# Chunked causal linear attention with a routed expert layer: a reordered start, the state's part of y as two products with q stationary behind y's transposes, and the state by column tiles

## The chip, the core and the metric

The kernel runs on one core of one Trainium2 chip, as one launch. The metric is the device time of that launch in microseconds (us), the median over runs. The core has a matrix engine (PE, with its weight loads listed apart as PEld), a vector engine (DVE), a scalar engine (ACT), a general engine (POOL) and SyncE (SP), which here only issues DMAs. The engines run their own instruction streams in order and meet at semaphores. Each stream of this kernel is written by hand, so what stands behind a waiting instruction on its engine waits too.

## The reference

`x` is 4 sequences of 1024 tokens of width 256. After a layer norm, three things are added: `x` itself, a causal linear attention with 16 heads of width 16, and a top-1 routed expert layer (8 experts, 256 to 1024 to 256).

```python
xn = _layernorm(x, axis=-1)
x = x + _L0_attn_ref(xn, w_attn, w_proj) + _L0_ffn_ref(xn, gate_w, gate_b, expert_bias, w1, b1, w2, b2)
...
q, k, v = jnp.split(qkv, 3, axis=2)                  # phi(a) = elu(a) + 1 is applied to q and k
def step(carry, blk):                                # over chunks of 128 tokens
    S, z = carry
    q_c, k_c, v_c = blk
    scores = jnp.einsum('bhcd,bhkd->bhck', q_c, k_c)
    scores = jnp.where(mask, scores, 0.0)
    num = jnp.einsum('bhck,bhke->bhce', scores, v_c) + jnp.einsum('bhcd,bhde->bhce', q_c, S)
    den = scores.sum(-1) + jnp.einsum('bhcd,bhd->bhc', q_c, z)
    S = S + jnp.einsum('bhkd,bhke->bhde', k_c, v_c)
    z = z + k_c.sum(axis=2)
    return ((S, z), (num, den))
y = num / (den[..., None] + 1e-06)
```

The expert layer picks one expert per token and adds `relu(xn @ w1[e] + b1[e]) @ w2[e] + b2[e]`.

## The kernel before

**Stages.** The kernel has three stages. In the first, from 0 to 20.6 us, the attention weights `wall` (WF in the code) are squared, summed over all rows on PE, and an exponent for their scale (SV) is derived; WF is then written as a high and a low float16 part (WA). The second stage is a software pipeline over 32 chunks of 128 tokens (4 sequences of 8 chunks, `CPB` = 8), whose step p works on chunks p to p-5; it also converts the expert weights to float16 pairs (two quarters a step: `w_max` on DVE, `w_scale` and `w_hi` on ACT, `w_lo` on POOL) and finds the routing. The third, from about 298 us to the end, is the expert layer: 39 slots, gathered, multiplied and scattered. The change leaves the third stage as it is.

**A chunk c in the second stage.** POOL and DVE normalise it (`sums`, `na`, `nn_begin`, `nn_end`, `nb`), ACT and POOL split it into float16 parts (`xh` L1051, `xl` L1204), PE transposes them (`xt` L359), ACT copies (`xTc` L1057), and PE multiplies to q and k with features on the partitions (`qk` L376) and to v and the gate (`vg` L392). ACT and DVE apply phi (`relu` L1065, `exp` L1069, `phi` L707, into QK), PE transposes k (`ktr` L399), POOL masks q to even and odd heads (`km` L1211). PE forms the scores (`scores` L416, 8 products in float32 on strips of 32 rows, four banks), DVE masks them (`s_mask` L713, four times), and PE multiplies with v into bank 5 with the head's 16 outputs and its denominator on the partitions (`pv` L445, 16 products on strips of 32 columns). ACT copies that to YT1 (`y1` L1094), PE transposes it to tokens on the partitions (`yt1` L472, bank 2), DVE divides (`y` L729, L731, L735), PE transposes back (`yt2` L478), ACT copies (`y2` L1100), PE projects (`pr` L486), DVE adds the residual (`res` L741).

**The state.** The running state of a sequence is kept in bank 6. `st` (L459) adds k transposed times v: two products of the full 128 by 128 array with 136 columns, so that blocks of different heads are computed too. DVE copies it times a head mask to T32 (`t32` L722). `inter` (L429) adds the state's part to y in bank 5: four products, T32 stationary and q streaming (128 columns each). It stands in front of `pv` of the same chunk, which adds to the same bank. The first chunk of a sequence has no `inter`, the last no `st`: 28 of each.

**Order.** One step p of PE runs: `scores(p-3)`, `st(p-3)`, `ktr(p-2)`, `xt(p-1)`, `yt1(p-4)`, `inter(p-3)`, `qk(p-1)`, `yt2(p-4)`, `vg(p-1)`, `pr(p-4)`, `pv(p-3)`. In every fourth step two small products for an expert's scale are added: `mx` (L511) before `yt1` and `mxa` (L521) before `qk`. One step of DVE runs: `phi(p-2)`, two `s_mask(p-3)`, `largest` in every fourth step, `y(p-4)`, `scale` in every fourth step, two `s_mask(p-3)`, `t32(p-3)`, `nb(p)`, `w_max`, a routing piece, `res(p-4)`, `sums` and `na` for chunk p+2, `w_max`. A step of ACT ends with `y2(p-4)`, `xh(p)`, `relu(p-1)`, `exp(p-1)`. POOL runs `km(p-2)`, then in even steps `nn_end` (eight instructions on 128 by 2 elements), `w_lo`, `xl(p)`, `w_lo`, and in odd steps `nn_begin`.

## Time and profile before

| what | value |
|---|---|
| median of 3 runs | 521.93 us (519.39 to 522.41) |
| the profiled execution's own time | 522.73 us, span 520.9 us |
| PE busy | 484.3 us, 93% of the span |
| DVE busy | 405.9 us, 78% |
| ACT busy | 279.2 us, 54% |
| POOL busy | 271.6 us, 52% |
| first stage, until `qk(0)` starts | 20.58 us |
| 27 steps, `qk` start 42.74 to 255.84 | 213.10 us, 7.89 us a step |
| mean granted TensorE clock | 0.971 |

An instruction's row gives its start, its duration, the engine, the line of the code, and in brackets how long the engine had been idle before it and who ended that. Durations on PE overlap, because the matmuls are pipelined: what one of a row of products costs is the distance from its start to the next one's. The chain of waits, listed in order of time, has this distance as its second column. A float32 product appears as two records, so that x8 are four products; a transpose of float32 appears as one, and float16 as one.

### The profile page before, as it was taken

Reading aid. Unit: us, or ns where it says so; the run is one execution under the profiler, and the core shown is the slowest. Engines: PE = TensorE matmul, PEld = TensorE weight load, DVE = VectorE, ACT = ScalarE, POOL = GpSimd, SP = SyncE. Lnnn points to the kernel's source line nnn. Section 1 sums busy time; section 2 is a strip of 40 time slices with the busy share of each in tenths; the row PEclk is TensorE's granted clock in tenths of the full one; section 3 lists DMA queues with packets and bytes.
Section 4 is the critical chain, followed back from the end, with each engine's and each line's share of the span. In section 5 each row is a group of like instructions: output and inputs, shape, how many; then the busy total and the mean of one; then the engine's idle time right before and its main releaser. Section 6 shows DMA issues by size and latency. Waiting matters only on the chain.

```text
span 520.9 us, 17449 instructions
## 1 busy us (share of the span) xinstructions
PE 484.3 (93%) x6071; PEld 395.8 (76%) x6071; DVE 405.9 (78%) x885; ACT 279.2 (54%) x535; POOL 271.6 (52%) x469
## 2 busy tenths in 40 slices
PE   4489999999999999999997499999999999999996
PEld 1378888788887888778875388888888888888884
DVE  2778889999899998999878547767768676677775
ACT  0346888788778787878885033333333333333331
POOL 3444766667766677766754533443534534433322
PEclk9679999999999999999998789999999999999999
DMA  8413556566466565573452431222122212220000
GB/s 272 156 57 99 164 172 211 162 190 202 154 205 179 175 205 179 159 223 129 161 166 102 142 93 62 69 66 79 59 63 72 66 57 82 63 69 23 28 15 1
DMA packets 34160, 62.88 MB, mean 121 GB/s; under 512 B 5661, under 2 KB 10014, under 8 KB 33952
## 3 DMA queue, kind: packets, MB, share of 16 engines
q1 hardware_dynamic: 29088, 49.17, 29.7%
q0 software_dynamic: 4992, 12.60, 8.0%
q8 instruction: 55, 0.90, 0.7%
q14 instruction: 25, 0.20, 0.1%
HBM read 51.00 MB, written 13.50 MB: 124 GB/s over the span
## 4 chain that ended last, share of the span: by engine, by line
PE 82%; DVE 5%; POOL 4%; issue 4%; ACT 3%; DMA 2%; DVEq 0%; POOLq 0%; ACTq 0%
PE ps L601 20%; PE ps L614 20%; PE ps L376 7%; PE ps L416 6%; PE ps L445 5%; PE ps L486 5%; PE ps L459 4%; PE ps L429 3%; PE ps L392 3%; PE ps L472 2%; PE ps L570 2%; PE ps L399 1%; PE ps L359 1%; PE ps L349 1%; PE ps L478 1%
## 5 line engine op out<-in xcount | busy, mean ns | idle before, releaser
L601 PEld LDWEIGHTS ps<-AR,W 128*128 x1872 | 131.6, 99 | 40.0 <-issue 1.1
L601 PE MATMUL ps<-AR,W 128*128 128x128 f16 x1872 | 155.9, 221 | 0.9 <-ACT AR L1148 0.9
L614 PE MATMUL ps<-W,ST 128*128 x624 | 150.4, 326 | 0.3 <-DVE ST L1008 0.3
L1157 ACT ACTIVATE ST<-ST 128x512 f16<-128x512 f32 x78 | 49.2, 630 | 112.0 <-DVE ST L996 107.3
L996 DVE SCALAR_TENSOR_TENSOR ST<-ps,TAs,B1S 128x512 f32<-128x512 f32 x78 | 58.4, 748 | 51.5 <-PE ps L601 48.3
L1305 POOL DMA_INDIRECT out<-AR x39 | 39.8, 1021 | 103.9 <-DVE AR L1028 99.6
L1245 POOL TENSOR_TENSOR W<-ST,W 128x512 f16<-128x512 f32 x64 | 74.3, 1161 | 28.8 <-ACT W L1107 28.1
L713 DVE TENSOR_TENSOR AR<-ps,CT 128x512 f32<-128x512 f32 x128 | 82.0, 683 | 4.4 <-PE ps L416 4.2
L1300 POOL DMA_INDIRECT AR<-scr,AR x39 | 49.9, 1279 | 34.6 <-issue 14.3
L1008 DVE SCALAR_TENSOR_TENSOR ST<-ST 128x512 f16<-128x512 f32 x78 | 53.6, 687 | 15.7 <-ACT ST L1157 15.3
L376 PE MATMUL ps<-xT,WA 128*128 128x128 f16 x768 | 50.7, 225 | 3.1 <-ACT xT L1057 3.1
L376 PEld LDWEIGHTS ps<-xT,WA 128*128 128x128 f16 x768 | 46.7, 101 | 4.7 <-ACT xT L1057 4.4
L614 PEld LDWEIGHTS ps<-W,ST 128*128 128x128 f16 x624 | 48.3, 98 | 2.0 <-issue 0.4
L1115 ACT ACTIVATE ST<-ST,SC 128x512 f32<-128x512 f32 x64 | 46.4, 725 | 0.0
L1148 ACT ACTIVATE AR<-ps 128x512 f16<-128x512 f16 x39 | 23.2, 595 | 41.5 <-PE ps L570 39.3
L1204 POOL TENSOR_TENSOR XR<-AR,XR 128x256 f16<-128x256 f32 x32 | 23.4, 732 | 38.8 <-ACT XR L1051 38.8
L748 DVE TENSOR_REDUCE MX<-ST 128x1 f32<-128x512 f32 x64 | 42.6, 665 | 0.0
L1211 POOL TENSOR_TENSOR AR<-AR,CT 128x512 f32<-128x512 f32 x32 | 33.3, 1042 | 16.0 <-DVE AR L707 15.8
L1107 ACT ACTIVATE W<-ST 128x512 f16<-128x512 f32 x64 | 40.4, 631 | 1.1
L416 PE MATMUL ps<-AR 32*128 32x256 f32 x512 | 38.1, 412 | 1.0 <-DVE XR L741 1.0
L486 PE MATMUL ps<-AR 128*128 128x256 f32 x128 | 35.1, 397 | 3.0 <-ACT AR L1100 3.0
L445 PE MATMUL ps<-AR 128*32 128x128 f32 x1024 | 35.4, 280 | 0.0
(149 smaller groups left out, 765.9 us busy)
## 6 DMA issues: line engine op xcount, KB each, us to landing
ST<-in_w SPq DMA_DIRECT2D x128, 256.0 KB, 4.2
scr<-XR SPq DMA_DIRECT2D x32, 256.0 KB, 2.2
XR<-in_x SPq DMA_DIRECT2D x32, 128.0 KB, 4.6
AR<-in_b SPq DMA_DIRECT2D x1, 1024.0 KB, 5.0
AR<-in_wall SPq DMA_DIRECT2D x1, 776.0 KB, 4.5
AR<-scr,AR POOLq DMA_INDIRECT x39, 3.6
out<-AR POOLq DMA_INDIRECT x39
ST<-in_cst SPq DMA_DIRECT2D x1, 576.0 KB, 4.9
```

Source lines behind the costliest of these rows:

```text
L376: a = e.matmul(PS[0][:, j * 128:(j + 1) * 128], WA[:, wl, k, j * 128:(j + 1) * 128], x_part(c, xl_, k), start=(n == 1), stop=(n == 6))
L416: a = e.matmul(PSC[r][:, g * 256:(g + 1) * 256], QK[c % 2][rows, 256 + g * 128:384 + g * 128], QM[c % 2][rows, g], start=True, stop=True)
L445: a = e.matmul(PS[5][32 * b:32 * b + 32, j * 128:(j + 1) * 128], V32[c % 2][:, 8 * g + 4 * i + b, :], S32[2 * i + t][:, (2 * g + o) * 128: ...
L486: a = e.matmul(PS[2][:, 256:512], YT2[:, k * 128:(k + 1) * 128], WPF[:, k, :], start=(k == 0), stop=(k == 1))
L601: a = e.matmul(dst, W[:, off:off + 57472][:, bass.ds(place_of(s), 128)], XT16[s % 2][:, xl * 256 + k * 128:xl * 256 + (k + 1) * 128], star ...
L614: a = e.matmul(PS[4 + s % 2][:, 0:w], src[h % 4][:, fs], W[:, off:off + 57344 + w][:, bass.ds(place_of(s), w)], start=(f == 0 and w == 512 ...
L713: e.tensor_tensor(S32[r].rearrange("p (b n) -> p b n", b=4), PSC[r][:, :].rearrange("p (b n) -> p b n", b=4), msk, ALU.mult).then_inc(s_[r ...
L996: e.scalar_tensor_tensor(H32[h % 2].rearrange("p (f n) -> p f n", f=4), PS[h % 4][:, :].rearrange("p (f n) -> p f n", f=4), TAs[:, :, 0][: ...
L1008: e.scalar_tensor_tensor(HL2[h % 4], H32[h % 2], 0.0, HH[h % 4], ALU.max, ALU.subtract).then_inc(v_hl, 1)
L1157: e.activation(HH[h % 4], H32[h % 2], ACT.Relu).then_inc(a_hh, 1)
L1245: e.tensor_tensor(lo_, src, hi, ALU.subtract).then_inc(p_wlo, 1)
L1300: e.indirect_dma_start(XG[s % NG], None, scr, bass.IndirectOffsetOnAxis(ids[:, s:s + 1], 0), bounds_check=NT - 1, oob_is_err=False).then_i ...
```

## The change

**The start.** The first two chunks of `x` are loaded before the weights, and the weights in two halves with a semaphore each. DVE squares one half and ACT the other, to bfloat16, and PE sums them in bfloat16 with a stationary of ones in that type. The maximum is one reduction over two neighbouring banks, and the exponent is found in three more instructions instead of eight. WA is written in two pieces (columns 0 to 511 for `qk`, 512 to 775 for `vg`). `nb(0)` stands ahead of the reduction.

**The state.** `st` is now eight products of 34 columns on strips of 32 array columns, which leave out the blocks between different pairs of heads, and it stands behind `pv` at the end of the step. `t32` spreads the 34 columns over four blocks times a mask that has a DMA of its own (MH), and runs one step later.

**The state's part of y.** `inter` is now two products with q stationary and T32 streaming (136 columns each), which add to bank 2 behind `yt1` of the same chunk, one step later than before. `y` waits for it. Since q lives longer, it has three buffers (QT) beside two for k (KK). `pv` no longer adds to `inter`'s result.

```diff
-            e.dma_start(WF, wall).then_inc(d_wall, 16)
             load_x(0)
+            load_x(1)
+            for k in range(2):
+                e.dma_start(WF[:, k, :], wall[:, k, :]).then_inc(d_wall[k], 16)
             e.dma_start(CT[:, :], cst).then_inc(d_cst, 16)
-            load_x(1)
             e.dma_start(TRI, tri).then_inc(d_tri, 16)
+            e.dma_start(MH, cmh).then_inc(d_mh, 16)
...
-            e.wait_ge(p_ones, 1)
-            e.wait_ge(v_sq, 1)
-            for n0, n1, bank in ((0, 512, 3), (512, 776, 4)):
-                for k in range(2):
-                    a = e.matmul(PS[bank][:, 0:n1 - n0], ONF, SQ[:, k, n0:n1], start=(k == 0), stop=(k == 1))
+            e.wait_ge(p_one16, 1)
+            for k in range(2):
+                if k == 0:
+                    e.wait_ge(v_sq, 1)
+                else:
+                    e.wait_ge(a_sq, 1)
+                for i in range(2):
+                    a = e.matmul(PS[3 + i][:, 0:388], one16[:, :], SQ[:, k, i * 388:(i + 1) * 388],
+                                 start=(k == 0), stop=(k == 1))
             a.then_inc(t_sq, 1)
...
                 e.wait_ge(S["t32"], n_state(c - 1))
-                e.wait_ge(S["y1"], c)
                 for g in range(2):
-                    for i in range(2):
-                        j = 2 * g + i
-                        a = e.matmul(PS[5][:, j * 128:(j + 1) * 128], T32[:, g, 4 * i:4 * i + 4, :],
-                                     QK[c % 2][:, g * 128:(g + 1) * 128], start=(j == 0), stop=True,
-                                     skip_group_check=True)
+                    a = e.matmul(PS[2][:, g * 256:(g + 1) * 256].rearrange("p (h e) -> p h e", h=8)[:, :, 0:17],
+                                 QT[c % 3][:, g * 128:(g + 1) * 128], T32[:, g], start=False, stop=True,
+                                 skip_group_check=True)
                 a.then_inc(S["in"], 1)
...
                 for g in range(2):
-                    a = e.matmul(PS[6][:, g * 136:(g + 1) * 136], KT32[c % 2][:, g * 128:(g + 1) * 128],
-                                 V32[c % 2][:, 8 * g:8 * g + 8, 0:17], start=(c % CPB == 0 and g == 0),
-                                 stop=True, skip_group_check=True)
+                    for b in range(4):
+                        h = 8 * g + 2 * b
+                        a = e.matmul(PS[6][32 * b:32 * b + 32, g * 34:(g + 1) * 34],
+                                     KT32[c % 2][:, g * 128 + 32 * b:g * 128 + 32 * b + 32],
+                                     V32[c % 2][:, h:h + 2, 0:17], start=(c % CPB == 0 and g == 0),
+                                     stop=True, skip_group_check=True)
                 a.then_inc(S["st"], 1)
...
                 if on(p - 3):
                     scores(p - 3)
-                    st(p - 3)
...
                 if on(p - 4):
                     yt1(p - 4)
-                if on(p - 3):
-                    inter(p - 3)
+                    inter(p - 4)
...
                 if on(p - 3):
                     pv(p - 3)
+                    st(p - 3)
...
-                e.tensor_tensor(T32[:, :, :, 0:17], PS[6][:, 0:272].rearrange("p (g h e) -> p g h e", g=2, h=8),
+                if c == 0:
+                    e.wait_ge(d_mh, 16)
+                e.tensor_tensor(T32.rearrange("p g (b h) e -> p g b (h e)", b=4),
+                                PS[6][:, 0:68].rearrange("p (g o n) -> p g o n", g=2, o=1).broadcast_to((128, 2, 4, 34)),
                                 mh, ALU.mult).then_inc(S["t32"], 1)
...
                 e.wait_ge(S["yt1"], c + 1)
+                if n_inter(c) > 0:
+                    e.wait_ge(S["in"], n_inter(c))
...
                     s_mask(p - 3, 3)
-                    t32(p - 3)
+                if on(p - 4):
+                    t32(p - 4)
...
+                if p == 0:
+                    e.wait_ge(v_sv, 1)
+                    wa_hi(slice(0, 512))
                 if on(p - 1):
+                    if p == 1:
+                        e.wait_ge(v_sv, 2)
                     relu(p - 1)
                     exp(p - 1)
```

On PE, one step of the pipeline, from `pv` to the next `qk`, read before as follows (ps5 and ps2 are the banks of y, ps6 that of the state; L445 is `pv`, L416 `scores`, L459 `st`, L399 `ktr`, L472 `yt1`, L429 `inter`, L376 `qk`):

```order
L445 MATMUL ps<-AR 32x128 [waits s_s0,s_s1,s_y1,s_vh]
...
L416 MATMUL ps<-AR 128x256 [waits s_s2,s_s3,s_s1,s_res,s_s0,s_km]
L416 MATMUL ps<-AR 128x256 x7
L459 MATMUL ps<-AR 128x136 [waits s_t32,s_vh,s_kt]
L459 MATMUL ps<-AR 128x136
L399 MATMUL ps<-CT,AR 128x128 [waits s_phi]
...
L472 MATMUL ps<-CT,AR 128x128 [waits s_res,s_s0,s_y1]
L472 MATMUL ps<-CT,AR 128x128 x3
L429 MATMUL ps<-AR 128x128 [waits s_y1,s_t32]
L429 MATMUL ps<-AR 128x128 x3
L376 MATMUL ps<-xT,WA 128x128 [waits s_kt,s_xTc]
```

The same stretch of PE after the change (L461 is `pv`, L478 `st`, L435 `scores`, L418 `ktr`, L492 `yt1`, L445 `inter`, L393 `qk`):

```order
L461 MATMUL ps<-AR 32x128 x7
L478 MATMUL ps<-AR 32x34 [waits s_t32,s_vh,s_kt]
L478 MATMUL ps<-AR 32x34 x7
L435 MATMUL ps<-AR 128x256 [waits s_s2,s_s3,s_s1,s_res,s_s0,s_km]
L435 MATMUL ps<-AR 128x256 x7
L418 MATMUL ps<-CT,AR 128x128 [waits s_phi]
...
L492 MATMUL ps<-CT,AR 128x128 [waits s_res,s_s0,s_y1]
L492 MATMUL ps<-CT,AR 128x128 x3
L445 MATMUL ps<-AR 128x8x17 [waits s_t32]
L445 MATMUL ps<-AR 128x8x17
L393 MATMUL ps<-xT,WA 128x128 [waits s_kt,s_xTc]
```

`st` has moved from between `scores` and `ktr` to between `pv` and `scores`; `inter` has two rows' worth of products fewer and no wait for `y1`.

On DVE, the middle of a step after the change (L729 is `s_mask`, L750 to L756 are `y`, L740 is `t32`, L673 `nb`):

```order
L729 TENSOR_TENSOR AR<-ps,CT 128x512 [waits s_pv,s_sc] x2
L750 TENSOR_SCALAR DN<-ps 128x16 [waits s_in,s_yt1]
L752 RECIPROCAL DN<-DN 128x16 [waits dv]
L756 TENSOR_TENSOR AR<-ps,DN 128x256 [waits s_yt2,dv]
L729 TENSOR_TENSOR AR<-ps,CT 128x512 [waits s_pv,s_sc] x2
L740 TENSOR_TENSOR AR<-ps,AR 128x272 [waits s_in,s_st]
L673 TENSOR_SCALAR AR<-XR,mv,rsn 128x256 [waits s_xl,s_nn]
```

The order of kinds is that of before; new is that the first instruction of `y` waits for `inter` (s_in) as well as for `yt1`.

On DVE at the program's start, after the change (L660 and L667 are `sums` and `na` of chunks 0 and 1, L673 is `nb(0)`, L686 the reduction of the sums of squares, L699 the low part of WA):

```order
L660 BN_STATS st<-XR 128x6 [waits s_na,d_x1]
L667 BN_AGGR mv<-st 128x2 [waits s_sums]
L682 TENSOR_TENSOR AR<-AR 128x776 [waits d_wall0]
L673 TENSOR_SCALAR AR<-XR,mv,rsn 128x256 [waits s_nn]
L686 TENSOR_REDUCE nv<-ps 128x1 [waits t_sq]
L689 TENSOR_SCALAR nv<-nv 128x1 [waits dv]
L691 TENSOR_SCALAR ni<-nv 128x1 [waits dv]
L694 TENSOR_SCALAR SV<-ni 128x1 [waits dv]
L696 TENSOR_SCALAR SV<-SV 128x1 [waits v_sv]
L699 SCALAR_TENSOR_TENSOR WA<-AR,SV,WA 128x2x512 [waits a_wa]
L699 SCALAR_TENSOR_TENSOR WA<-AR,SV,WA 128x2x264 [waits a_wa]
```

Before, the squares of the whole WF stood first, then `sums` and `na`, the two reductions, eight small instructions, `nb(0)`, and one low part of all 1552 columns.

## Rows read from the trace of the kernel before

**Rows 1.** The page, part 1: busy us (share of the span) xinstructions
```profile
PE 484.3 (93%) x6071; PEld 395.8 (76%) x6071; DVE 405.9 (78%) x885; ACT 279.2 (54%) x535; POOL 271.6 (52%) x469
```

**Rows 2.** Chain of waits, one step of PE: start us, us to the next
```profile
121.71 1.34 PE ps L376 x24
...
124.88 1.01 PE ps L445 x32
...
126.96 0.66 PE ps L459 x4
...
128.07 0.45 PE ps L472 x4
128.51 0.89 PE ps L429 x8
```

**Rows 3.** Windows between starts of qk: length, busy us (count) by engine, clock, DMA
```profile
74.06:97.39 23.33, 22.35 (x307) 18.38 (x307) 21.70 (x50) 18.34 (x39) 15.29 (x30) 1.00 0.60 184
97.39:137.51 40.12, 40.09 (x539) 33.95 (x540) 37.16 (x91) 32.57 (x67) 28.59 (x66) 1.00 0.62 192
```

**Rows 4.** Timeline of DVE, one step: start us, us, line, operands, idle before
```profile
118.68 0.68 DVE L707 SCALAR_TENSOR_TENSOR AR<-ps,AR 128x512 f32<-128x512 f32 x1
...
120.85 0.17 DVE L729 TENSOR_SCALAR DN<-ps 128x16 f32<-128x16 f32 x1 [0.23 <-PE ps L472]
...
123.23 1.21 DVE L656 TENSOR_SCALAR AR<-XR,mv,rsn 128x256 f32<-128x256 f32 x1
...
126.41 0.68 DVE L707 SCALAR_TENSOR_TENSOR AR<-ps,AR 128x512 f32<-128x512 f32 x1
```

**Rows 5.** Line L656 (nb): ns min/median/max; and its last long one, timeline
```profile
L656 DVE TENSOR_SCALAR AR<-XR,mv,rsn x32: 400/403/1230, 15.1 to 257.4; 128x256 f32<-128x256 f32 x32
...
249.66 1.21 DVE L656 TENSOR_SCALAR AR<-XR,mv,rsn 128x256 f32<-128x256 f32 x1
```

**Rows 6.** Chain of waits, mxa (L521) ahead of a qk
```profile
137.21 0.31 PE ps L521 x2
```

**Rows 7.** Chain of waits in the first stage
```profile
0.74 4.53 DMA AR<-in_wall
...
7.22 5.53 PE ps L349 x8
12.77 0.69 DVE nv L665
...
15.24 1.59 ACT WA L1047
...
20.58 2.76 PE ps L376 x24
23.36 0.70 ACT AR L1065
```

**Rows 8.** Timeline of the first stage: na(1), end of nn_end, WA's low part, nb(1)
```profile
8.20 0.18 DVE L650 BATCH_NORM_AGGREGATE mv<-st 128x2 f32<-128x6 f32 x1
...
12.12 0.20 POOL L1182 TENSOR_TENSOR rsn<-rsn,nr 128x2 f32<-128x2 f32 x1
...
16.86 1.83 DVE L684 SCALAR_TENSOR_TENSOR WA<-AR,SV,WA 128x1552 f16<-128x1552 f32 x1 [1.34 <-ACT WA L1047]
...
20.45 0.49 DVE L656 TENSOR_SCALAR AR<-XR,mv,rsn 128x256 f32<-128x256 f32 x1
```

**Rows 9.** List of DMA issues: KB each, median us to landing
```profile
XR<-in_x SPq DMA_DIRECT2D x32, 128.0 KB, 4.6
...
GBE<-in_eb SPq DMA_DIRECT2D x1, 4.0 KB, 3.1
```

**Rows 10.** Windows in the start: length, busy by engine, PEclk, DMA share, GB/s
```profile
32.00:34.00 2.00, 2.00 (x21) 1.45 (x18) 0.98 (x2) 0.39 (x2) 1.04 (x1) 0.72 0.41 136
```

**Rows 11.** Chain of waits, y of the last two chunks
```profile
280.11 0.64 PE ps L472 x4
...
286.42 0.27 DVE DN L731
```

More of the change, by code:

```diff
@@ L75, in sem @@
             return ctx.enter_context(nc.semaphore(name))
-        PS = [ctx.enter_context(nc.psum_tensor(f"ps{i}", [128, 512], F32)) for i in range(8)]
+        PSS = {i: ctx.enter_context(nc.psum_tensor(f"ps{i}", [128, 1024 if i == 3 else 512], F32))
+               for i in (0, 1, 2, 3, 5, 6, 7)}
+        PS = [PSS[i][:, 0:512] if i != 4 else PSS[3][:, 512:1024] for i in range(8)]
         W = sb("W", [128, E * 8192], F16)
@@ L123, in sv @@
             return SV[:, i:i + 1].bitcast(F32)
-        QK = [ar(512 * i, 512) for i in range(2)]
+        QT = [ar(256 * i, 256) for i in range(3)]
+        KK = [ar(768, 256), ar(1632, 256)]
+        QK = [ar(256 * (i % 3), 2 * ((768, 1632)[i % 2] - 256 * (i % 3))).rearrange("p (s n) -> p s n", s=2)[:, :, 0:256]
+              for i in range(6)]
         QM = [ar(2048 + 512 * i, 512).rearrange("p (g o n) -> p g o n", g=2, o=2) for i in range(2)]
@@ L257, in program @@
         d_scr = [sem(f"d_scr{i}") for i in range(R)]
-        d_wall, d_wp, d_cst, d_tri, d_small, d_cst2, d_b2 = (
-            sem(n) for n in ("d_wall", "d_wp", "d_cst", "d_tri", "d_small", "d_cst2", "d_b2"))
+        d_wall = [sem(f"d_wall{k}") for k in range(2)]
+        d_mh = sem("d_mh")
+        d_wp, d_cst, d_tri, d_small, d_cst2, d_b2 = (
+            sem(n) for n in ("d_wp", "d_cst", "d_tri", "d_small", "d_cst2", "d_b2"))
         d_wm = [sem(f"d_wm{i}") for i in range(4)]
@@ L447, in pv @@
                                              S32[2 * i + t][:, (2 * g + o) * 128:(2 * g + o + 1) * 128],
-                                             start=(c % CPB == 0 and j == 0), stop=True, skip_group_check=True)
+                                             start=(j == 0), stop=True, skip_group_check=True)
                 a.then_inc(S["pv"], 1)
@@ L679, in vector @@
[L679 to L684 removed]
+            e.tensor_scalar(SV[:, 0:1], ni[:, 0:1], EXP, None, ALU.bitwise_and).then_inc(v_sv, 1)
@@ L685, in vector @@
+            e.wait_ge(v_sv, 1)
+            e.tensor_scalar(SV[:, 1:2], SV[:, 0:1], -1.0, 244.0 * 2 ** 23, ALU.mult, ALU.add).then_inc(v_sv, 1)
+            for i, n in enumerate((slice(0, 512), slice(512, 776))):
+                e.wait_ge(a_wa, i + 1)
+                e.scalar_tensor_tensor(WA[:, 1, :, n], WF[:, :, n], sv(0), WA[:, 0, :, n],
+                                       ALU.mult, ALU.subtract).then_inc(v_wa, 1)
             e.wait_ge(d_small, 48)
@@ L706, in phi @@
                 e.wait_ge(S["exp"], c + 1)
-                e.scalar_tensor_tensor(QK[c % 2], PS[0][:, :], 1.0, QK[c % 2], ALU.min, ALU.add).then_inc(S["phi"], 1)
+                e.scalar_tensor_tensor(QK[c % 6], PS[0][:, :].rearrange("p (s n) -> p s n", s=2), 1.0, QK[c % 6], ALU.min, ALU.add).then_inc(S["phi"], 1)
             def s_mask(c, r):
@@ L1060, in relu @@
                 e.wait_ge(S["qk"], c + 1)
+                if c == 0:
+                    e.wait_ge(v_wa, 2)
                 if c >= 2:
                     e.wait_ge(S["sc"], c - 1)
-                if n_inter(c - 2) > 0:
-                    e.wait_ge(S["in"], n_inter(c - 2))
-                e.activation(QK[c % 2], PS[0][:, :], ACT.Relu, scale=sv(1)).then_inc(S["relu"], 1)
+                if n_inter(c - 3) > 0:
+                    e.wait_ge(S["in"], n_inter(c - 3))
+                e.activation(QK[c % 6], PS[0][:, :].rearrange("p (s n) -> p s n", s=2), ACT.Relu, scale=sv(1)).then_inc(S["relu"], 1)
             def exp(c):
@@ L1365 @@
     cst[:, C_T] = i
+    cmh = ((i[:, None] // 16) == np.arange(136)[None] // 17).astype(np.float32)
     nc = _bacc.Bacc("TRN2", target_bir_lowering=False, num_devices=1)
```

87 lines of the change are left out of this document (43 added, 44 removed).

## The prediction

> **What bounds the kernel now.** I read the page first: PE is busy for 93% of the span and DVE for 78% [rows 1], but the share is a mean over three stages, so the chain of waits was read next, stage by stage. In the middle of the second stage it consists of PE alone: a step of 7.70 us, from one `qk` at 121.71 to the end of `inter` at 129.40, where the next starts [rows 2]. The reader should add it up: `qk` to the start of `st` 5.25 (`qk`, `yt2`, `vg`, `pr`, `pv`, `scores`), `st` 0.66, `ktr` and `xt` 0.45 (to 128.07), `yt1` 0.45, `inter` 0.89.
>
> The windows then show how far that holds. From 42.74 to 255.84 lie 27 steps in seven stretches. In four of them (18 steps) PE has no idle time, as in 40.09 of 40.12 us; in the three stretches around a sequence's end (9 steps, 23.3 us each) it is busy for 22.3 only [rows 3]. There the chain runs through POOL's `nn_end`, `nb` on DVE and ACT.
>
> The second engine is close behind. One DVE step, `phi` to `phi`, took 7.73 us, of which 0.23 was waiting, for `yt1` [rows 4]. It had a long `nb`: 1.21 us against a median of 0.403 [rows 5]; it overlaps a subtraction of POOL (`w_lo`). The trace has seven such, every fourth step, the last at 249.66 [rows 5]. Without it a DVE step is 7.73 - 0.81 = 6.92, with its wait.
>
> The first stage is a chain: weights landed, squares, 5.53 of float32 products for the sums, then small DVE instructions, the high and the low part of WA, `xl`, and `qk(0)` at 20.58 [rows 7].
>
> **The start.** The float32 products no longer bind; what does is the normalisation of chunks 0 and 1, as `nb(0)` now stands ahead of the reduction. The second load of `x` is issued at about 1.2 and lands 4.6 later by the median of such loads [rows 9], at 5.8. With `sums` and `na`, 0.65, that is 6.45. From the end of `na(1)` at 8.38 to the end of `nn_end` at 12.32 [rows 8] are 3.94, so 10.4; `nb(0)` 0.4, 10.8. The squares by then are long summed (weights landed at about 6.5, 0.9 for a half, then four bfloat16 products). The reduction of 776 columns is 0.69 for 512 and about 0.35 for the rest [rows 7], 11.85; three small instructions at 0.19, 12.4. The high part of 1024 of 1552 elements is 1.59 x 0.66 = 1.05 [rows 7], 13.5; the low part 1.83 x 0.66 = 1.21 [rows 8], 14.8 with latencies. So `qk(0)` starts at 14.85, 5.7 earlier. But `relu(0)` stands on ACT behind `xh(1)`, and this behind `nb(1)`, which ended 2.25 after WA's low part (18.69 to 20.94) [rows 8]; with its second piece of 0.65 first, `nb(1)` ends at 17.7, `xh(1)` at 18.2, while `qk(0)` is done at 17.6. So `relu(0)` starts at 18.2 instead of 23.36 [rows 7]: **-5.2**. If `x` lands in 3.1, as one of the smallest loads did [rows 9], this is -6.7. The extra mask load (70 KB) hides behind the stage; its reader, `t32(0)`, comes 20 us later.
>
> **PE's step.** *inter.* One float32 product of 128 columns costs 0.89 / 4 = 0.22 [rows 2]. Two of 136 cost 2 x 0.22 x 136/128 = 0.48; the upper bound is `st` of before, also two products of 136 columns, 0.66 [rows 2]. I take 0.48, since the difference of 0.18 is the step from strips of rows (`scores`) to the full array, which `inter` behind `yt1` doesn't have. It is **-0.41** on PE, 28 times. *st.* The 0.18 stays and moves to `ktr`, now right behind `scores`. The eight narrow products have no row. Above, `pv` takes 1.01 for 16 products on the same strips with 128 columns [rows 2], so 0.51 for eight; below, by columns, 0.51 x 34/128 = 0.13. I take 0.50, near the row, because the cost of 32 records in `pv` (0.032 each) can't be seen to fall with the columns. `st` is then 0.50 + 0.18 against 0.66: nothing. PE's step is 5.25 + 0.50 + 0.18 + 0.45 + 0.44 + 0.48 = 7.30.
>
> The Trainium skill ("TensorE: Matmul & The Clock Gate", section "Wait — 56ns, not 53.3ns?") has a floor for this: the distance between starts never falls below about 25 ns however few the columns. No row here shows such narrow products. By it 16 records are 0.40 and the step 7.20; by the row it is 7.30.
>
> **What of it arrives.** DVE's `y` now waits for `inter`, and behind `y` queue two `s_mask`, `t32`, `nb`, and through `nb` ACT's `xh`, `relu` and `exp`. But `st` is gone from ahead of `ktr`. Before, `y` started 1.49 after `phi`'s end (119.36 to 120.85) [rows 4]. Now `ktr` starts as `phi` ends, and 0.45 + 0.44 + 0.48 and latencies give 1.47. So DVE's step is unchanged: 6.92, or 7.73 with a long `nb`. By kinds of step:
> - light (two of four): PE 7.30 is longer than DVE 6.92; gain 0.40.
> - with a long `nb` (one of four): DVE sets 7.73; gain 0. `nb` keeps its distance to POOL's `w_lo`, since both hang on `phi`, so it stays one of four.
> - with `mx` and `mxa` (one of four): `mxa` costs PE 0.31 more [rows 6]. DVE's `largest` follows its first two `s_mask`, and gives its result about 1.8 after `phi`, while PE is through `inter` at 1.5; PE waits 0.3. Gain about 0.15.
>
> That is 0.95 in four steps, over 18 steps **-4.3**. In the nine steps at a sequence's end PE is not the bound: 0. `st` behind `pv` needs `t32(p-4)`, which DVE does ahead of `nb`, long before; `y1` and `vh` on ACT wait for `pv` there and `vh` now for `st` too, beside which `y1`'s 0.6 runs.
>
> **The end of the stage.** `yt1` of the last two chunks leads to `y` on the chain [rows 11]. There `inter` was done beforehand and is now in between: 2 x 0.48, **+1.0**. ACT sets the steps between, so a shorter `inter` gives nothing there. The third stage is the same code.
>
> **Sum.** -5.2 - 4.3 + 1.0 = -8.5. The profiled execution's own time, 522.73 (span 520.9), becomes 514.2. The median of the runs is 0.8 lower, 521.93, so 513.4 is predicted.
>
> **Rivals.**
> - *Nothing from the loop.* DVE, POOL and ACT hold a step at 7.7 to 7.8, as they already do in the nine steps [rows 3]. For it: DVE is idle for 0.23 of 7.73 in the long step. Against: without a long `nb` it has 0.78. Time: 521.9 - 5.2 + 1.0 = 517.7. Chance 0.18.
> - *All of the loop.* The later `inter` and earlier `ktr` shift `nb` off `w_lo`, and the nine steps gain about 0.3 too: 18 x 0.40 + 9 x 0.3 = 9.9. For it: all seven long ones have one phase. Time: 521.9 - 5.2 - 9.9 + 0.5 = 507.3. Chance 0.2.
> - *The clock rises later.* The granted clock rose from 1.2 to 2.4 GHz between 32 and 34 us, where it is 0.72 in the mean, with PE busy throughout [rows 10]; the 5.5 us of float32 products ahead are gone. If the rise stays where it is in time, one more step runs at 1.2 GHz: its `qk` takes 2.76 instead of 1.34 [rows 2, 7], with the transposes about 2.2. Time: 513.4 + 2.2 = 515.6. Chance 0.08.
> - *Slower: the clock falls inside the loop.* PE now idles up to 0.4 in DVE's steps. At 1.2 GHz a step of 7.3 becomes 14.6. Two such steps more than undo the 8.5; for slower by over 1% it takes two. Against it: the stretches with 22.35 busy of 23.33 show a granted clock of 1.00 [rows 3]. Time with two: 513.4 + 14.6 = 528. Chance 0.04.
>
> **Range and chances.** The forecast has 0.5, with its own range 510 to 516.5: with narrow products at 0.13 PE's light step is 0.37 shorter still, but then DVE's 6.92 holds, 3.4 less in all; `x` landing early is 1.5 less; `inter` at 0.66 is 1.6 more. The range reaches to both neighbours, 506.5 to 518. Measurements can't tell less than about 1%, 5.2 us, from no change: faster by more is below 516.7. Faster: 0.46 of the forecast, 0.2, 0.07 and 0.03 of the first rival, 0.76. Same: 0.2. Slower: 0.04.
>
> **What the new profile would show.** `qk(0)` at about 15 and `relu(0)` at 18.2; the first windows at 2.4 GHz about 5 us earlier; light steps of 7.3 and long ones of 7.7; `st` at 0.50 and `inter` at 0.48 in the chain; PE waiting for `phi` at `ktr` in the long steps and for `largest` at `mxa`; `y` started by `inter` after a wait of about 0.2. It would be wrong if `x` landed after the weights, if `y` waited for more than 0.5, or if `nb` were long in another share of the steps.

## The result and the profile after

Median of 7 runs 517.6 us (515.47 to 519.1), beside 521.64 (519.18 to 522.41, 7 runs) of the kernel before: ratio 0.9934, 95% interval 0.9906 to 0.9962. The gain is 4.0 us; 8.5 were forecast. It is real, since the interval leaves out 1, but smaller than the 1% that the prediction took as its line for "faster" (516.7). The profiled execution took 517.73 (span 515.9; before 522.73 and 520.9). That of before is 1.1 us above its median, so differences read from the two traces come out larger than the medians' 4.0. Of e7's four runs below, one of 512.36 us is left out, as it is over 1.5% above the fastest.

The page after, parts 1 and 4 (busy us; shares of the chain that ended last), to be held against [rows 1]:

```profile
PE 463.5 (90%) x6291; PEld 376.1 (73%) x6291; DVE 405.0 (78%) x881; ACT 279.2 (54%) x537; POOL 259.7 (50%) x468
...
PE 55%; DVE 24%; issue 9%; POOL 6%; ACT 4%; DMA 1%; DVEq 0%; POOLq 0%; ACTq 0%
```

PE's work did fall, by 20.8 us. The same line of the page before began with PE 82%, DVE 5%: the chain has moved to DVE.

To see where the time went, the span is cut at `phi(3)`, `phi(30)` and the first product of the third stage. Windows (length, busy us and count by engine, clock, DMA) between these cuts, before:

```profile
47.52:260.18 212.66, 209.74 (x2850) 176.38 (x2846) 195.91 (x465) 171.63 (x352) 146.37 (x309) 1.00 0.58 180
260.18:298.87 38.69, 26.66 (x296) 20.20 (x292) 27.66 (x80) 19.93 (x38) 19.56 (x21) 0.87 0.41 139
```

and after:

```profile
39.50:254.12 214.62, 195.93 (x3046) 161.12 (x3042) 195.27 (x465) 170.48 (x352) 145.68 (x309) 1.00 0.57 178
254.12:293.95 39.83, 26.10 (x312) 19.72 (x307) 27.10 (x80) 19.84 (x38) 20.09 (x22) 0.81 0.42 135
```

The start gained 8.0 (47.52 to 39.50), the 27 steps of the loop lost 2.0 (212.66 to 214.62) although PE's busy time in them fell by 13.8, the drain (from `phi(30)` to the first product of the third stage) lost 1.1 (38.69 to 39.83), and the third stage is the same (222.0 and 221.9). Sum -5.0, as the spans say.

Of the 2.0 that the loop lost, 1.9 lie in the nine steps around a sequence's end (`phi(7)` to `phi(10)` and the like: 71.56 us before, 73.44 after). The other 18 steps took 141.1 before and 141.2 after.

The chain of waits inside one step of after (start us, us to the next) shows what sets the step now:

```profile
87.81 0.61 DVE AR L723
88.42 0.04 issue
88.47 0.44 PE ps L418 x2
88.90 0.22 PE ps L376 x4
89.13 0.61 PE ps L492 x4
89.74 0.48 PE ps L445 x4
...
90.31 0.19 DVE DN L750
```

`phi` (L723) releases `ktr` (L418), then come `xt` (L376), `yt1` (L492) and `inter` (L445), and only then `y` (L750). On one engine the chain counts from the end of one piece to the end of the next, so the 0.61 of `yt1` holds a wait as well as its work; the section on why the prediction was wrong takes it apart. DVE's timeline (in brackets the idle time before an instruction, and who ended it), a light step and the step with the long `nb` (L673):

```profile
103.56 0.68 DVE L723 SCALAR_TENSOR_TENSOR AR<-ps,AR 128x512 f32<-128x512 f32 x1
104.16 1.28 DVE L729 TENSOR_TENSOR AR<-ps,CT 128x512 f32<-128x512 f32 x2
...
106.14 0.17 DVE L750 TENSOR_SCALAR DN<-ps 128x16 f32<-128x16 f32 x1 [0.57 <-PE ps L445]
...
111.02 0.68 DVE L723 SCALAR_TENSOR_TENSOR AR<-ps,AR 128x512 f32<-128x512 f32 x1
...
113.60 0.17 DVE L750 TENSOR_SCALAR DN<-ps 128x16 f32<-128x16 f32 x1 [0.70 <-PE ps L445]
...
116.21 1.23 DVE L673 TENSOR_SCALAR AR<-XR,mv,rsn 128x256 f32<-128x256 f32 x1 [0.15 <-POOL rsn L1216]
...
119.40 0.68 DVE L723 SCALAR_TENSOR_TENSOR AR<-ps,AR 128x512 f32<-128x512 f32 x1
```

From `phi`'s end (104.24) to `y` (106.14) are 1.90 us; before it was 1.49 [rows 4]. The wait of 0.23 has become 0.57 and 0.70. In the long step `nb` waits as well, 0.15 for POOL. Waits of DVE from 60 to 250 us (total, times, longest), after:

```profile
DVE DN L750 <- PE ps L445: 12.3, 18, 0.7
```

and before, where `res` (L741) waited for `pr` too:

```profile
DVE XR L741 <- PE ps L486: 5.1, 11, 0.7
DVE DN L729 <- PE ps L472: 3.9, 18, 0.4
```

### The profile page after: what moved, and what is told of

It reads as the page before. It is cut to its first block, busy times and chain, and to the rows that moved or that the text cites. A ratio compares the mean times of both kernels' runs of the same rounds, so it can differ in the third digit from the quotient of the medians.

```text
span 515.9 us, 17895 instructions
## 1 busy us (share of the span) xinstructions
PE 463.5 (90%) x6291; PEld 376.1 (73%) x6291; DVE 405.0 (78%) x881; ACT 279.2 (54%) x537; POOL 259.7 (50%) x468
## 4 chain that ended last, share of the span: by engine, by line
PE 55%; DVE 24%; issue 9%; POOL 6%; ACT 4%; DMA 1%; DVEq 0%; POOLq 0%; ACTq 0%
PE ps L621 21%; PE ps L634 20%; DVE AR L729 5%; DVE MX L769 4%; DVE AR L723 2%; DVE AR L673 2%; PE ps L492 2%; PE ps L590 2%; POOL W L1279 2%; DVE st L660 2%; PE ps L445 1%; PE ps L507 1%; PE ps L393 1%; PE ps L461 1%; PE ps L418 1%
## 5 line engine op out<-in xcount | busy, mean ns | idle before, releaser
L621 PEld LDWEIGHTS ps<-AR,W 128*128 x1872 | 132.2, 99 | 39.8 <-issue 1.1
L729 DVE TENSOR_TENSOR AR<-ps,CT 128x512 f32<-128x512 f32 x128 | 81.9, 682 | 3.6 <-PE ps L435 3.5
L1336 POOL DMA_INDIRECT AR<-scr,AR x39 | 40.2, 1032 | 31.0 <-issue 21.6
L393 PE MATMUL ps<-xT,WA 128*128 128x128 f16 x768 | 50.8, 225 | 4.0 <-DVE WA L699 2.2
L393 PEld LDWEIGHTS ps<-xT,WA 128*128 128x128 f16 x768 | 45.3, 101 | 7.0 <-ACT xT L1082 4.5
L1238 POOL TENSOR_TENSOR XR<-AR,XR 128x256 f16<-128x256 f32 x32 | 22.1, 691 | 45.5 <-ACT XR L1076 45.5
L435 PE MATMUL ps<-AR 32*128 32x256 f32 x512 | 38.2, 413 | 5.9 <-DVE XR L762 5.8
L461 PE MATMUL ps<-AR 128*32 128x128 f32 x1024 | 35.4, 280 | 0.0
```

Of the source, the lines that this page charges most:

```text
L393: a = e.matmul(PS[0][:, j * 128:(j + 1) * 128], WA[:, wl, k, j * 128:(j + 1) * 128], x_part(c, xl_, k), start=(n == 1), stop=(n == 6))
L461: a = e.matmul(PS[5][32 * b:32 * b + 32, j * 128:(j + 1) * 128], V32[c % 2][:, 8 * g + 4 * i + b, :], S32[2 * i + t][:, (2 * g + o) * 128: ...
L621: a = e.matmul(dst, W[:, off:off + 57472][:, bass.ds(place_of(s), 128)], XT16[s % 2][:, xl * 256 + k * 128:xl * 256 + (k + 1) * 128], star ...
L729: e.tensor_tensor(S32[r].rearrange("p (b n) -> p b n", b=4), PSC[r][:, :].rearrange("p (b n) -> p b n", b=4), msk, ALU.mult).then_inc(s_[r ...
```

## The experiments

**Theory A:** in the loop, PE no longer sets the step; DVE's order `phi`, two masks, `y`, two masks, `nb` does, and `y` stands still in it until `inter` is through. **Rivals:** B, PE's work still sets the step and something else took the gain; D, PE's restart behind an idle time holds it up; E, ACT's or POOL's chain. All kernels below are the changed one with the edit shown, unless another base is named. Each ratio is to runs of before made beside that kernel, whose medians lay between 519.97 and 521.88, so kernels are better compared by ratio than by median. Steps are distances between starts of `phi`; the four are the same four in every kernel (in after from 103.56 on): light, with the long `nb`, light, with `mx`. The loop is `phi(3)` to `phi(30)`, the drain what follows up to the third stage; both are read from one profiled execution.

| kernel | median us (range, runs) | ratio to before, 95% | four steps | loop | drain (clock) |
|---|---|---|---|---|---|
| before | 521.64 (519.18-522.41, 7) | | 7.85 7.73 7.86 8.02 | 212.7 | 38.7 (0.87) |
| changed | 517.6 (515.47-519.1, 7) | 0.9934, 0.9906-0.9962 | 7.46 8.38 7.52 8.16 | 214.6 | 39.8 (0.81) |
| e1 start only | 512.75 (512.62-514.2, 4) | 0.987, 0.9835-0.9906 | 7.94 7.60 7.89 8.02 | 212.4 | 37.6 (0.91) |
| e2 loop only | 523.37 (521.92-524.68, 9) | 1.0056, 1.0036-1.0076 | 7.45 8.37 7.52 8.17 | 214.6 | 40.0 (0.80) |
| e9 half of inter | 512.57 (511.5-515.85, 4) | 0.987, 0.9822-0.9918 | 7.26 8.33 7.45 8.00 | 211.2 | 39.4 (0.81) |
| e3 y behind third mask | 512.97 (507.69-514.41, 4) | 0.9832, 0.9767-0.9897 | 7.26 7.98 7.45 7.64 | 206.8 | 43.6 (0.71) |
| e6 w_lo behind xl | 514.37 (511.54-516.15, 4) | 0.9875, 0.9829-0.9921 | 7.53 7.56 7.53 8.08 | 209.2 | 44.1 (0.69) |
| e7 both | 507.42 (503.84-508.98, 3) | 0.9724, 0.9652-0.9795 | 7.25 7.34 7.53 7.69 | 202.6 | 41.1 (0.78) |
| e12 both, products in the drain | 506.94 (505.81-507.13, 4) | 0.9727, 0.9692-0.9762 | 7.26 7.33 7.54 7.69 | 202.9 | 40.3 (0.96) |
| e19 third mask, products in the drain | 511.32 (510.98-512.94, 4) | 0.9812, 0.9774-0.985 | 7.26 8.06 7.45 7.61 | 207.3 | 40.5 (0.95) |
| e10 inter alone | 524.12 (520.87-526.42, 9) | 1.0061, 1.003-1.0091 | 7.88 8.35 7.52 8.29 | 218.1 | 41.7 (0.84) |
| e16 narrow st, old place | 513.4 (513.08-516.4, 4) | 0.9861, 0.9815-0.9907 | 7.64 7.77 7.77 7.98 | 211.5 | 38.2 (0.85) |

### Which half of the change

e1 is the kernel before with the new start alone, e2 the kernel before with the new `st`, `inter` and their places alone.

> Only the reordered start, with the loop of before. Theory A (the start's lead is worth its 6.8 us, and the loop of the change loses what it could have gained, by DVE's wait for the product): the lead stays, the loop keeps 7.88 a step, 6.5 to 7 us less than before, about 514.8. Rival B (an earlier start can't help because the loop is held by something with its own timetable, such as the weights' loads; the loop of the change is worth the 4 us): the lead is lost within the first ten steps, 520 to 522.

> Only the new state products (st by column tiles behind pv, two products of inter behind yt1, three buffers of q), with the start of before. Theory A: slightly slower than before, by 2 to 3 us (27 steps of 7.95 instead of 7.88, and 1 us at the end), about 524. Rival B: 4 us faster than before, about 517.6.

The two halves add up: e1's ratio is worth -6.8 us, e2's +2.9, together -3.9, and the whole change -3.4 by its ratio, -4.0 by its medians. The start is worth more than forecast, and the loop part costs time. Both came as expected from theory A (6.5 to 7 less, 2 to 3 more). e1, with less of the change, is faster than all of it.

### Is it y's wait

e9 leaves out the second of `inter`'s two products (the state's part of heads 8 to 15), so that `y` waits about 0.24 less:

```diff
-                for g in range(2):
+                for g in range(1):
                     a = e.matmul(PS[2][:, g * 256:(g + 1) * 256].rearrange("p (h e) -> p h e", h=8)[:, :, 0:17],
...
```

> The changed kernel with only the first of the two products of the state's part of y (heads 0 to 7; the part for heads 8 to 15 is left out, so that the output is not complete), everything else as changed: a dose test of y's wait. y then starts some 0.22 to 0.24 us earlier behind yt1. Theory A (y's wait for inter lies on the path in every step but the first of each stretch): the step falls by 0.2 us or more in most steps, the loop by 4 to 7 us (214.6 to 208 to 211), and the time to 511 to 514 us. Rival B (y's wait only fills time that DVE has; the step is set elsewhere, by DVE's and PE's sum or by TensorE's restart): loop and time as in the changed kernel within 1 us.

The loop fell by 3.4 us (4 to 7 expected), the median by 5. The first light step gives back 0.20 of 0.24 and the `mx` step 0.16; the second light step gives 0.07 and the step with the long `nb` only 0.05. In that one the first mask now starts 0.78 after `phi`'s start, behind the scores, and not 0.60. So the wait is on the path, but not in every step.

e3 lets DVE do the third mask while PE is at `inter`:

```diff
-                if on(p - 4):
-                    y(p - 4)
-                scale(p)
                 if on(p - 3):
                     s_mask(p - 3, 2)
+                if on(p - 4):
+                    y(p - 4)
+                scale(p)
+                if on(p - 3):
                     s_mask(p - 3, 3)
```

> The changed kernel with DVE's y (and scale) moved behind the third score mask of the step, so that 0.65 us of masking stands between the second mask and the wait for inter. Theory A (DVE sets the step, and 0.6 to 0.7 of it is the wait of y for inter): light steps go from 7.46 to about 7.0, where PE takes over, long ones from 8.38 to 7.75; 27 steps lose 9 to 13 us, time 505 to 509. Rival C (the step is set by the chain nb, xh, relu, exp over ACT, or by POOL, whatever DVE waits for): within 1.5 us of the changed kernel, 516 to 519.

Waits of DVE from 60 to 250 us, in e3:

```profile
DVE XR L762 <- PE ps L507: 2.6, 7, 0.4
DVE DN L750 <- PE ps L445: 0.5, 1, 0.5
```

12.3 us of waiting became 0.5, and the loop fell from 214.6 to 206.8 with the same instructions on all engines: theory A holds for the loop, and B falls. 3.0 of the 7.8 lie in the nine steps around a sequence's end. The steps came to 7.26 and 7.98, not to the 7.0 and 7.75 expected, and the total fell by less than the loop; that is taken up below. Rival E falls as the only bound, since no edit of ACT or POOL was made.

### The long nb

e6 takes POOL's first `w_lo` of even steps behind `xl`:

```diff
-                for n in q[:1]:
+                for n in q[:1] if p % 2 else ():
                     w_lo(n)
                 if on(p):
                     xl(p)
-                for n in q[1:]:
+                for n in q[1:] if p % 2 else q:
```

> The changed kernel with POOL's first weight subtraction of even steps moved behind xl, so that nb on DVE doesn't fall beside it. Theory D (the long nb, 1.2 us instead of 0.4, comes from that subtraction and is paid in full, as DVE has no slack left): no nb over 0.7 us, the steps of 8.38 become 7.5, about 5.5 us less than the changed kernel, 512. Rival: POOL's km and nn_end come later and nb waits for them instead: no gain or slower, 517 to 520.

Line L673 (`nb`; ns min/median/max) in the changed kernel, then in e6:

```profile
L673 DVE TENSOR_SCALAR AR<-XR,mv,rsn x32: 401/406/1225, 9.0 to 252.0; 128x256 f32<-128x256 f32 x32
```

```profile
L673 DVE TENSOR_SCALAR AR<-XR,mv,rsn x32: 400/402/413, 8.8 to 246.6; 128x256 f32<-128x256 f32 x32
```

The long `nb` is gone, its step went from 8.38 to 7.56, and `y` waited for `inter` as long as before (12.3 us again). It is a second, separate cost. e7 makes both edits:

> The changed kernel with both of the earlier edits of order: DVE's y and scale behind the third mask, and POOL's first low half of even steps behind xl. Theory A (in the loop the changed kernel is bound by DVE's cycle phi, mask, y, nb with PE's ktr, yt1 and inter in the middle of it; y's wait and the long nb are two separate additions to it): the two gains add up. y behind the third mask took 7.8 us out of the loop (phi to phi 214.6 to 206.8), the other edit took the long nb out of DVE (6 us of busy time) and about 3 us out of the total; together phi(3) to phi(30) is 200 to 204 us and the time 508 to 511 us, less if the clock holds in the drain. Rival B (one of the two waits only hides in the other): the loop stays at 206 to 208 and the time at 512 to 514 us. Rival C (what the loop gives the drain takes back, by the lower clock there): the loop falls to 200 to 204 but the time stays at 512 to 514 us, with a granted clock of 0.5 to 0.8 in the last 25 us before the first expert product.

Loop 202.6: the gains of 7.8 and 5.4 add up to 12.0 of 13.2. The kernel is 2.8% faster than before (interval 2.1 to 3.5%).

### What each loop edit is worth

e10 puts `st` back to two products of 136 columns (still behind `pv`):

```diff
-                    for b in range(4):
-                        h = 8 * g + 2 * b
-                        a = e.matmul(PS[6][32 * b:32 * b + 32, g * 34:(g + 1) * 34],
-                                     KT32[c % 2][:, g * 128 + 32 * b:g * 128 + 32 * b + 32],
-                                     V32[c % 2][:, h:h + 2, 0:17], start=(c % CPB == 0 and g == 0),
+                    a = e.matmul(PS[6][:, g * 136:(g + 1) * 136], KT32[c % 2][:, g * 128:(g + 1) * 128],
+                                 V32[c % 2][:, 8 * g:8 * g + 8, 0:17], start=(c % CPB == 0 and g == 0),
...
```

> The changed kernel with the state's products back at full width (two products of 136 columns a chunk in place of sixteen of 34 on 32-column strips; the state's mask then a plain product over 272 columns), everything else as changed: so the change without its edit of st. PE's work per step is then 0.35 to 0.5 us more. Theory A (DVE's cycle sets the step, PE has slack of 0.3 to 0.5 us before ktr): the loop stays within 2 us of the changed kernel's 214.6 us and the time is 517 to 520 us, so that st's 0.13 us in place of 0.66 bought almost nothing. Rival B (PE still sets the step, as the prediction had it, and only something else took the gain): 27 steps of 0.35 to 0.5 us more, loop 224 to 228, time 527 to 531 us.

The loop grew by 3.5 us, 0.13 a step, between the two expectations: one of the four steps pays 0.42 and another 0.13. The total rose by more (1.3% by the ratios), as `phi(3)` came 1.5 later and the drain was 1.9 longer in the profiled execution; the cause of these two is open. So in the loop the new `inter` and place of `st` cost 5.7 us against e1, and the narrow products give 3.5 back.

e16 is e1 with the narrow products at `st`'s old place, between `scores` and `ktr` (same diff the other way round, and `t32` in two instructions):

> The kernel before with the new start (as in the first run of this series, 512.8 us) and with the state's products by column tiles at their OLD place, between the scores and ktr; inter in its old form and place, nothing else. Theory F (the old place of st is covered: yt1 may only write its bank when DVE's first mask has read the scores there, about 1.07 us behind the scores' end, and st 0.66, ktr 0.22 and xt 0.22 took 1.10): taking 0.53 us out of st gives at most 0.1 us a step, since TensorE then waits at yt1 for the mask or at ktr for phi; loop from 212.4 to 209 to 213 us, time 509 to 513.5 us. Rival B (TensorE's own work is what sets the step, so that 0.5 us less of it arrives): 18 steps of 0.5 less, 9 us off: loop 203 to 205, time 503 to 505 us.

Chain of waits, one light step from `st` to `yt1`, in e1 (L470, L410, L368, L483), then in e16 (L472, L410, L368, L486):

```profile
110.97 0.66 PE ps L470 x4
111.63 0.22 PE ps L410 x2
111.85 0.22 PE ps L368 x4
112.07 0.45 PE ps L483 x4
```

```profile
111.07 0.27 PE ps L472 x16
111.33 0.37 PE ps L410 x2
111.70 0.22 PE ps L368 x4
...
111.93 0.63 PE ps L486 x4
```

`st` became 0.39 shorter, and the pieces of `ktr` and `yt1` 0.15 and 0.18 longer: 0.06 arrived, 0.9 us in the loop. The old place was nearly free. `yt1` may write its bank only when the first mask has read the scores there. In all 25 steps from `phi(5)` to `phi(29)` of e16, `yt1` starts 0.10 after that mask's end; in e1 it is 0.10 to 0.19 in all but three steps (0.31), so there was little to gain. Rival B (9 us) is out. Whether `ktr`'s 0.15 comes from its wait for `phi` (it starts 0.10 after `phi`'s end) or from standing behind products on strips is open.

Two attempts at `st` alone with `st` behind `pv` (e11: old `inter` ahead of `pv`; e13: old `inter` at its old place, `t32` moved behind `phi`) missed what theory A expected of them, by 13 to 18 us and 8 to 14 us. They made new waits of their own, and so don't tell what it is worth there:

> The changed kernel with the state's part of y back in its old form (four products with the state's mask stationary into the bank of pv, ahead of pv, and no wait of y for them), the state by column tiles kept: so the change without its edit of inter. PE's work per step is 0.4 us more than in the changed kernel, but none of it lies between phi and y. Theory A (the changed kernel's step is set by phi, ktr, yt1, inter, y): y starts 0.45 to 0.5 us earlier behind phi, the step is 7.5 to 7.65 us, phi(3) to phi(30) 203 to 208 us, and the time 508 to 513 us, less than with both edits. Rival D (it is not inter but TensorE's start behind an idle time, 0.2 us more for ktr and 0.16 us more for yt1, that holds the step up): the loop is 211 to 214 us and the time 515 to 518 us. Rival B (PE's work sets the step): 0.4 us a step more than the changed kernel, 528 us.

> The state by column tiles alone, once more, with the state's part of y (four products, old form) at its old place behind yt1, where it covers ACT's kt and xTc ahead of qk; DVE's t32 now stands behind phi, in the time in which DVE waits for the scores. So against the changed kernel only the edit of inter is undone. In the earlier form with inter ahead of pv, ACT's chain from pv's end (y1, vh, lg, the scaled weights, kt, xTc) to qk was the longest and the step was 8.1 us. Theory A (in the changed kernel y's wait for inter between phi and the masks sets the step, and TensorE's work no longer does): the step is 7.4 to 7.6 us, phi(3) to phi(30) 200 to 206 us (214.6 changed), and the time 505 to 511 us, though TensorE has 0.41 us more to do in each step than in the changed kernel. Rival E (ACT's chain sets it here too, since st no longer stands between pv and kt): the loop is 213 to 219 us and the time 517 to 524 us. Rival D (the restart of TensorE behind its wait at ktr, 0.2 and 0.16 us): loop 208 to 212, time 512 to 516.

e11 took 525.79 us (524.56 to 529.56): `inter` no longer covered ACT's `xTc` ahead of `qk`, and the loop was 218.4. e13 took 519.28 (518.39 to 520.62), loop 217.3: `t32` (0.50) delayed the first mask, and PE stood ahead of `yt1`. PE's timeline in e13:

```profile
104.92 0.44 PE L416 MATMUL ps<-CT,AR 128*128 128x128 f32 x2
...
105.98 0.63 PE L493 MATMUL ps<-CT,AR 128*128 128x128 f32 x4 [0.26 <-issue]
```

With `t32` in between, `yt1` starts 1.11 after `phi`'s end instead of 0.70, and again 0.10 after the first mask's end: it follows the mask. Rival E's numbers (loop 213 to 219, 517 to 524 us) came for e13, but this delay of the mask explains it without ACT; no run tells the two apart. Neither kernel judges rival D, the restart of PE; the rows speak against it, see the failed step below. Three more kernels removed the long `nb`: from e13, with `y` behind the third mask as well (e15: 518.83 us, loop 216.5), from e16 (e17: 511.59, loop 209.3) and from e1 (e18: 512.26, loop 210.7).

> The kernel of the row above (state by column tiles, the state's part of y in its old form and place) with the two edits of order: y and scale behind the third mask, POOL's first low half of even steps behind xl. Theory A: y waited for little there, so that the first edit gives nothing or costs up to 2 us, and the second takes the long nb out, 2 to 4 us: phi(3) to phi(30) 196 to 203 us, time 501 to 508 us, the fastest so far. Rival E (ACT's chain behind pv): both edits are off the path, and the time is that of the row above within 1 us.

> The kernel of the row above with POOL's first low half of even steps behind xl (no long nb on DVE). Theory F: TensorE's ring scores, mask, yt1, inter, qk sets the step, so that a shorter nb gives little: 0 to 3 us less than the row above. Rival G (DVE's work is as long as TensorE's now, so that what is taken from it arrives): 3 to 6 us less than the row above, time 505 to 508 us.

> The kernel before with the new start and POOL's first low half of even steps behind xl, the loop otherwise as before (full-width st, old inter). TensorE has no idle time there in 18 of 27 steps, so the forecast's reading says that a shorter nb gives nothing in these: loop 212.4 less 0 to 2 us, time 511 to 513 us. Against the row above it tells what the narrow products are worth once the long nb is gone. Rival G (DVE's long nb holds the loop before too): 3 us less, time 509 to 510 us.

That gave 0.8 (for both edits of e15), 2.2 and 1.7 us in the loop there, against 5.4 in the changed kernel: what DVE loses counts in full only where DVE sets the step.

### Where e3's gain went in the drain

e3's drain took 43.6 us against 39.8, at a granted clock of 0.71. e19 and e12 add, to e3 and e7, idle products behind the last `ktr`:

```diff
+            def warm(p):
+                if p > NC:
+                    e.wait_ge(S["kt"], NC)
+                    for _ in range(10):
+                        e.matmul(PS[0][:, 384:512], one16[:, :], one16[:, :], start=True, stop=True)
...
```

> The changed kernel with y behind the third mask (513.0 us, loop 206.8 us, from phi(30) to the first expert product 43.6 us where the changed kernel takes 39.8), and with ten or twenty more products of 128 columns per step on TensorE in the drain into a free bank, used by nothing. Theory C (the drain took back 4 us of the 7.8 by a granted clock of 0.5 to 0.8): the clock in the drain stays near 1.0, phi(30) to the first expert product is 39 to 40.5 us, and the time 508.5 to 510.5 us. Rival (the drain is longer for another reason, such as DVE's later y): 43 to 44.5 us, time 513 to 514 us.

> The kernel with both edits of order and, in the steps behind the last phi, ten or twenty more products of 128 columns per step on TensorE into a free bank, where it waits anyway (they compute nothing that is used). It is to be compared with the one without them. Theory C (the drain of the last chunks is lengthened by a granted clock that falls while TensorE waits): the clock stays at 1.0 or near it up to the placement, the stretch from the last qk to the first expert product goes from 39 to 40 us down to 33 to 35, and the time is 3 to 5 us less than without the products. Rival (the drain is a chain of DVE, ACT and the placement, and the clock only goes along): the time is the same or up to 1 us more, since the added products cost 0.5 to 1.1 us a step where they come ahead of yt1.

Windows from `phi(30)` to the first product of the third stage, e3 and then e19:

```profile
246.80:290.38 43.58, 29.60 (x312) 21.96 (x312) 26.82 (x81) 19.96 (x38) 19.77 (x22) 0.71 0.36 124
```

```profile
246.55:287.00 40.45, 27.60 (x382) 21.88 (x382) 26.84 (x81) 19.93 (x38) 19.93 (x22) 0.95 0.40 133
```

70 more records, and 2.0 us less PE time: the clock stayed up, and the drain was 3.1 us shorter. On e7 it was 0.8 (41.1 to 40.3), where 33 to 35 and 3 to 5 us in the total had been expected: that did not come, and with the idle products in it, a drain at a mean clock of 0.96 is still 40 us long. The ratios are alike (0.9832 and 0.9812, 0.9724 and 0.9727), so the totals don't show a gain. What did change is the spread: 507.7 to 514.4 became 511.0 to 512.9. The low clock is shown as the main part (3.1 of 3.8) of what e3's drain took longer than the changed kernel's, in one profiled execution; why the single runs differ in it is open. e7 and e12, alike by their ratios, are the fastest of the series, ahead of both kernels.

## Why the prediction was wrong, step by step

- **Where the 8.5 went.** The start gave 8.0 by `phi(3)` instead of 5.2, the drain cost 1.1 instead of 1.0, and the loop cost 2.0 where 4.3 had been forecast as a gain. Step by step, light steps gained 0.39 and 0.34 (0.40 forecast, right), the step with `mx` lost 0.14 (a gain of 0.15 forecast), the one with the long `nb` lost 0.65 (0 forecast), and the nine steps around a sequence's end lost 1.9 together (0 forecast).
- **The start (-5.2): right in kind, too small.** `relu(0)` starts at 16.58, not 18.2, so -6.8 against [rows 7]. The chain of waits in after:

```profile
0.74 2.14 DMA XR<-in_x
...
9.44 0.89 DVE nv L686
...
10.91 1.16 ACT WA L1072
12.09 1.14 DVE WA L699
...
16.58 0.68 ACT AR L1092
```

  The first chunk of `x` landed at 2.9 and the second, for which 5.8 was forecast, at 3.3, 2.1 after its issue; the prediction's variant with an early `x` said -6.7. POOL's `nn_end` took back 0.7 of it (4.32 to 9.00, 3.94 forecast). By `phi(3)` another 1.2 had come. The rival of the late clock fell: `qk(2)` ran at full speed at 28.10 (1.51 us), earlier than in [rows 10].
- **`inter` 0.48 a pair: right as a distance** (0.48 in the chain), but its result comes later, see below.
- **`st` 0.50 + 0.18: mis-sized.** In the chain of after:

```profile
253.77 0.13 PE ps L478 x16
```

  It took 0.13, the lower bound by columns; 0.50 was taken. The rule quoted from the Trainium skill ("TensorE: Matmul & The Clock Gate", section "Wait — 56ns, not 53.3ns?"), no start closer than about 25 ns, is not borne out here: sixteen records in 0.13 us are 8 ns apart in the mean (at 110.14 they start in fours, 7 ns apart within a four and 30 to 36 from one four to the next). Whether the 0.18 is there in `ktr` can't be told, as `ktr` stands behind its wait for `phi`: the distance from its start to that of `xt` is 0.28 instead of 0.22.
- **"So DVE's step is unchanged: 6.92 / 7.73": this step failed.** The estimate of 1.47 from `phi`'s end to `y` was 1.90, in the light step and in the long one. In the long one (`phi` ends at 111.70, `y` starts at 113.60), DVE and then PE:

```profile
111.61 0.68 DVE L729 TENSOR_TENSOR AR<-ps,CT 128x512 f32<-128x512 f32 x1
```

```profile
111.75 0.44 PE L418 MATMUL ps<-CT,AR 128*128 128x128 f32 x2 [0.22 <-DVE AR L723]
...
112.39 0.63 PE L492 MATMUL ps<-CT,AR 128*128 128x128 f32 x4
112.86 0.63 PE L445 MATMUL ps<-AR 128*128 128x136 f32 x4
```

  Two terms were left out. First, `yt1` does not start when `ktr` and `xt` are through (0.45 forecast) but 0.70 after `phi`'s end, 0.10 after the end of DVE's first mask (112.29), which must have read the bank that `yt1` writes. The wait stands in the list of `yt1`'s waits (s_s0), and the prediction did not price it; it is 0.10 to 0.12 in all steps from `phi(5)` to `phi(29)`, and e13 shows that `yt1` follows the mask. That is 0.25. Second, 0.44 and 0.48 are distances between starts, but `y` waits for the end of `inter`, which comes 0.63 after its start: 0.15 more. `yt1` to `inter` was 0.46, and `y` started 0.11 after `inter`'s end. So 0.70 + 0.46 + 0.63 + 0.11 = 1.90. The same four transposes took 0.61 from start to end in before, in a stream without a pause:

```profile
120.21 0.61 PE L472 MATMUL ps<-CT,AR 128*128 128x128 f32 x4
```

  So it is no restart of PE that makes them longer (rival D), but 0.02 at most. A light step is 7.46 to 7.52 (7.30 forecast), a long one 8.38 (7.73), one with `mx` 8.16 (about 7.87). A light step had slack on DVE for most of this, the long one had none, and the nine steps around a sequence's end, which the prediction left unchanged, pay as well: e3 gives 3.0 back there. The prediction named this sign itself: `y` waiting for more than 0.5. The split into the two terms is read from the rows; that `y`'s wait costs the loop time is shown by e9 and e3.
- **One long `nb` in four: right in the main.** Six of over 1.1 us are left of seven, at the same steps, and three of 0.67 to 0.72 came new (at 100.7, 164.6 and 228.5). Its 0.81 was counted into a step of 7.73; with `y` 0.43 later and `nb` waiting 0.15 for POOL that makes 8.31 of the 8.38.
- **The drain +1.0: right in kind** (+1.1), since `inter` of the last two chunks now stands in the chain. The agreement of the size is partly luck, since the two drains ran at different granted clocks (0.87 and 0.81):

```profile
274.17 0.48 PE ps L445 x4
...
280.14 0.48 PE ps L445 x4
```

- **The rivals.** "Nothing from the loop" gave 517.7, and 517.6 came. Its ground was half right: DVE does hold the step. But that the number fits is luck, by two errors: a start 2.8 better by `phi(3)` and a loop 2.0 worse. The clock in the loop stayed at 1.00, against the slower rival. My chance of 0.18 for this case was too low, because its only evidence against was a slack of 0.78 on DVE computed from the failed step.

## What to carry to other kernels

When two engines hand work back and forth within a step, cut the ring in which each waits for the other first, and only then the work of the busier one: 13.8 us less of PE time brought nothing while `y` stood behind `inter`, and one mask moved into that wait brought 7.8. When work is moved ahead of another engine's wait, go through every wait in its list, not the nearest alone (`yt1` waited for the mask, 0.25), and price the last piece by its row from start to end (0.63), not by the distance to the next start (0.48). Of a piece to be shortened, ask what the engine would wait for in its place.
